# First layer norm's rstd and shift: from four GpSimd instructions to seven ScalarE instructions

## What is computed

```
h = layernorm(x) * (1 + ca) + sa
x = x + ga * mamba(h)        # in_proj, conv, silu, x_proj, softplus, selective scan, gate, out_proj
h = layernorm(x) * (1 + cb) + sb
x = x + gb * moe(h)          # one shared expert, the best of 7 routed experts
layernorm(x) = (x - mean(x)) / sqrt(var(x) + 1e-05)
```

## Time and profile before

| | |
|---|---|
| median of 3 runs | 2424.81 us (2423.86 to 2426.68) |
| profiled execution, its own time | 2425.52 us |
| span of that execution in the profile | 2423.7 us |
| PE busy | 2129.3 us, 88% |
| DVE busy | 1948.4 us, 80% |
| POOL busy | 1979.4 us, 82% |
| ACT busy | 1346.9 us, 56% |

### The profile page before, as it was taken

How to read it: one execution, slowest core, us unless ns; L and a number is a source line. 1 busy time by engine, 2 the same in 40 slices (tenths; PEclk the granted TensorE clock), 3 DMA queues, 4 the chain that set the end, 5 groups by cost and what they waited for, 6 DMA issues and landing times. The chain is left out here.

```text
span 2423.7 us, 31216 instructions
## 1 busy us (share of the span) xinstructions
PE 2129.3 (88%) x7668; PEld 1007.6 (42%) x7669; DVE 1948.4 (80%) x2114; ACT 1346.9 (56%) x2391; POOL 1979.4 (82%) x858
## 2 busy tenths in 40 slices
PE   8859898988989898989898989889875779999998
PEld 3214343443434343434343334434332456666565
DVE  4889999999999999999999999999999832222222
ACT  4657666667585767666666667675745212222221
POOL 1999999999989999999998999999899445555553
PEclk9868999899989898989899899999887889999999
DMA  6433242424242324343242424242422512222221
GB/s 175 137 101 98 78 106 65 104 74 117 77 102 72 98 74 103 83 101 103 75 111 74 108 68 117 80 103 69 98 69 53 208 42 87 86 87 85 84 85 47
DMA packets 148360, 224.35 MB, mean 93 GB/s; under 512 B 47187, under 2 KB 84577, under 8 KB 144098
## 3 DMA queue, kind: packets, MB, share of 16 engines
q1 hardware_dynamic: 134818, 182.40, 28.8%
q0 software_dynamic: 13376, 40.12, 5.5%
HBM read 99.46 MB, written 31.45 MB: 54 GB/s over the span
## 5 line engine op out<-in xcount | busy, mean ns | idle before, releaser
L1279 POOL TENSOR_TENSOR ring<-ring,reps 128x2048 f32<-128x2048 f32 x256 | 1154.7, 4530 | 42.6 <-ACT state L865 42.6
L973 DVE TENSOR_TENSOR_SCAN ring<-dA,state,ring 128x512 f32<-128x512 f32 x768 | 929.7, 1262 | 13.5 <-ACT dA L850 9.2
L850 ACT ACTIVATE dA<-d_rep,a 128x512 f32<-128x512 f32 x1024 | 690.1, 686 | 433.1 <-DVE ring L973 426.4
L1272 POOL TENSOR_TENSOR ring<-u_rep,reps 128x2048 f32<-128x2048 f32 x96 | 436.2, 4544 | 44.6 <-PE bank L590 44.5
L960 DVE TENSOR_TENSOR ring<-u_ps,reps 128x2048 f32<-128x2048 f32 x160 | 360.5, 2269 | 8.8 <-issue 4.9
L590 PE MATMUL bank<-ring,spread 128*32 128x512 f32 x2048 | 283.2, 703 | 42.4 <-POOL ring L1279 37.8
L561 PE MATMUL bank<-n,w1s 128*128 128x512 f32 x512 | 266.1, 657 | 61.1 <-DVE delta L941 38.5
L973 DVE TENSOR_TENSOR_SCAN ring<-dA,ring 128x512 f32<-128x512 f32 x256 | 293.7, 1201 | 11.5 <-ACT dA L850 10.4
L1553 DVE TENSOR_TENSOR hid<-z,sg 128x512 f32<-128x512 f32 x70 | 48.4, 692 | 295.6 <-ACT sg L1530 295.6
L1468 PE MATMUL z<-ring,hT 128*128 x560 | 262.2, 612 | 3.6 <-issue 2.1
L516 PE MATMUL bank<-xin,w_in 128*128 128x512 f32 x512 | 244.9, 619 | 8.3 <-ACT xin L701 8.3
(11 more groups left out here) (237 smaller groups left out, 2456.7 us busy)
## 6 DMA issues: line engine op xcount, KB each, us to landing
d_rep<-delta SPq DMA_DIRECT2D x1024, 64.0 KB, 2.0
reps<-bc_rows SPq DMA_DIRECT2D x128, 256.0 KB, 6.3
u_rep<-us SPq DMA_DIRECT2D x384, 64.0 KB, 2.0
xres<-in_x SPq DMA_DIRECT2D x16, 512.0 KB, 3.6
token_rows<-xpad SPq DMA_DIRECT2D x32, 256.0 KB, 2.4
token_rows<-xres SPq DMA_DIRECT2D x16, 512.0 KB, 2.9
xin<-in_x SPq DMA_DIRECT2D x15, 512.0 KB, 9.4
ring<-in_w SPq DMA_DIRECT2D x7, 1024.0 KB, 14.5
```

The source lines that it names most:

```text
L850: nc.scalar.activation(dA[:, u % ABANK, :], d_rep[:, q, :], ACT.Exp, scale=t["a"][:, u:u + 1]).then_inc(da_ready, 1)
L973: nc.vector.tensor_tensor_scan(hs[:, s % RING, g, :], dA[:, u % ABANK, :], hs[:, s % RING, g, :], state[:, u:u + 1] if m else 0.0, ALU.mul ...
L1272: nc.gpsimd.tensor_tensor(hs[:, s % RING], u_rep[:, i % UBUF, :].unsqueeze(1).to_broadcast([P, NG, T]), b_rep[:, par, :].rearrange("p (g t ...
L1279: nc.gpsimd.tensor_tensor(hs[:, s % RING, :, :], hs[:, s % RING, :, :], c_rep[:, par, :].rearrange("p (g t) -> p g t", g=NG), ALU.mult).th ...
```

## The change

`rstd` and `shift` of the first layer norm are computed by ScalarE. `rstd` becomes `exp(-0.5 * ln(var + eps))`: an Ln with eps as its bias, an Exp with scale -0.5; the mean is negated by a Copy, and `shift` is made by four Copies of one column each, since their scale is a column of `rstd`. The new piece is V, at set 11, tile 0 of `evict`; piece R leaves `gps`. In the start, `deviation(0)` stands ahead of the silu of `c`, and `deviation(1)` behind the load of the exponential table. `mhalf` gets a wider tile, whose upper half holds eps. The list `transfers` is only broken into lines differently.

```
-            11: [[], [], [], [(('B', 2), -1)]],
+            11: [[(('V', 0), 2)], [], [], [(('B', 2), -1)]],
...
-            8: [(('IN', 13), 0), (('R', 0), 2), (('G0', 0), -1)],
+            8: [(('IN', 13), 0), (('G0', 0), -1)],
...
+            def deviation(f):
+                act.wait_ge(stats_ready, f + 1)
+                if known(f) and f == 0:
+                    act.wait_ge(zeroed, 5)
+                nc.scalar.activation(rstd[:], mv[:, :, 1], ACT.Ln, bias=eps[:, 0:1]).then_inc(rstd_step, 1)
+                nc.scalar.activation(mv[:, :, 0], mv[:, :, 0], ACT.Copy, scale=-1.0).then_inc(rstd_step, 1)
+                act.wait_ge(rstd_step, 3 * f + 2)
+                nc.scalar.activation(rstd[:], rstd[:], ACT.Exp, scale=-0.5).then_inc(rstd_step, 1)
+                act.wait_ge(rstd_step, 3 * f + 3)
+                for tt in range(TT):
+                    last = nc.scalar.activation(shift[:, tt:tt + 1], mv[:, tt, 0:1], ACT.Copy, scale=rstd[:, tt:tt + 1])
+                last.then_inc(shift_ready, 1)
...
+            exp_table()
             act.wait_ge(a_loaded, 16)
             nc.scalar.activation(t["a"][:], t["a"][:], ACT.Exp).then_inc(a_exp, 1)
+            deviation(0)
             act.wait_ge(c_loaded, 16)
             nc.scalar.activation(cs, cT, ACT.Silu).then_inc(c_silu, 1)
             normalize(0)
...
                     exp_table()
+                    deviation(1)
                     act.wait_ge(selectors, 1 + NF)
...
-            def rsqrt(f):
-                hold(pool, stats_ready, f + 1, held)
-                nc.gpsimd.tensor_scalar(mv[:, :, 1], mv[:, :, 1], EPS, None, ALU.add).then_inc(rstd_step, 1)
-                nc.gpsimd.tensor_scalar(mv[:, :, 0], mv[:, :, 0], -1.0, None, ALU.mult).then_inc(rstd_step, 1)
-                hold(pool, rstd_step, 3 * f + 2, held)
-                nc.gpsimd.tensor_tensor(rstd[:], mv[:, :, 1], t["mhalf"][:, 0:TT], ALU.pow).then_inc(rstd_step, 1)
-                hold(pool, rstd_step, 3 * f + 3, held)
-                nc.gpsimd.tensor_tensor(shift[:], mv[:, :, 0], rstd[:], ALU.mult).then_inc(shift_ready, 1)
...
-            rsqrt(0)
-            rsqrt(1)
```

More of the change, by code:

```diff
@@ L118, in fused_program @@
         mv2, rstd2, shift2 = sb("mv2", [P, TT, 2]), sb("rstd2", [P, TT]), sb("shift2", [P, TT])
+        eps = t["mhalf"][:, TT:TT + 1]
         xpad, us, res = t["xpad"], sb("us", [P, 2, KI, T]), sb("res", [P, 2, KI, T])
@@ L255, in fused_program @@
             15: []}
-        transfers = [('W2', 0), ('ACC2', 0), ('U', 5), ('D', 4), ('XR', 0), ('D', 6), ('U', 7), ('D', 5), ('D', 8), ('U', 10), ('WO', 0), ('D', 7),
-                     ('U', 13), ('D', 10), ('D', 9), ('BC', 0), ('X', 0), ('D', 11), ('ROWS', 0), ('D', 12), ('D', 13), ('D', 15), ('D', 14), ('LOG', 0),
-                     ('U', 15), ('D1', 0), ('U1', 2), ('D1', 2), ('D1', 1), ('D1', 3)]
+        transfers = [('W2', 0), ('ACC2', 0), ('U', 5), ('D', 4), ('XR', 0), ('D', 6), ('U', 7), ('D', 5), ('D', 8), ('U', 10), ('WO', 0), ('D', 7), ('U', 13), ('D', 10), ('D', 9),
+                     ('BC', 0), ('X', 0), ('D', 11), ('ROWS', 0), ('D', 12), ('D', 13), ('D', 15), ('D', 14), ('LOG', 0), ('U', 15), ('D1', 0), ('U1', 2), ('D1', 2), ('D1', 1), ('D1', 3)]
         FIRST_TRANSFERS = [("D", 0), ("D", 1), ("D", 2), ("U", 2), ("D", 3)]
@@ L802, in lump @@
                     logs(f, int(kind[1]))
+                elif kind == "V":
+                    deviation(f)
                 elif kind == "N":
@@ L1303, in body @@
                         do(item, c, m)
-            nc.gpsimd.memset(t["mhalf"][:], -0.5).then_inc(zeroed, 1)
+            nc.gpsimd.memset(t["mhalf"][:, 0:TT], -0.5).then_inc(zeroed, 1)
+            nc.gpsimd.memset(eps, EPS).then_inc(zeroed, 1)
             nc.gpsimd.memset(t["ident"][:], 0.0).then_inc(zeroed, 1)
@@ L1308, in _ @@
             nc.gpsimd.memset(xpad[:, :, 0:KCONV - 1], 0.0).then_inc(zeroed, 1)
-            pool.wait_ge(zeroed, 4)
+            pool.wait_ge(zeroed, 5)
             nc.gpsimd.affine_select(out=t["ident"][:], in_=t["ident"][:], compare_op=ALU.not_equal, fill=1.0,
@@ L1580, in build @@
                 "spread": spread, "gather": spread[:, 0, :], "state": sb("state", [P, NSET * NG]), "xpad": sb("xpad", [P, KI, T + KCONV - 1]),
-                "mhalf": sb("mhalf", [P, TT]),
+                "mhalf": sb("mhalf", [P, 2 * TT]),
                 "a": sb("a", [P, NSET * NG]), "cb": sb("cb", [P, KI]),
```

2 lines of the change are left out of this document (removed).

## The result

The changed kernel is slower, as forecast: 2438.15 us (median of 5, 2436.60 to 2439.48), where the kernel before ran 2424.77 us beside it. The ratio is 1.0054, 95% interval 1.0039 to 1.0069, so +13.4 us; forecast were +17.6 (2442.4 us). The profiled execution took 2439.48 us, its span is 2437.6 us, 13.9 more than before.

The account below looks back on a forecast made before the run. VectorE was taken as the bound, hanging on ScalarE at one point of the chunk. Loop 16.5 + start 2.3 - chunk 0's 1.2 = 17.6 us, giving 2442.4 us; range 2426 to 2450, the forecast's own 2438 to 2449.2.

Parts of the forecast that it names:

- The path: Chunks 1 to 13: V delays ScalarE's table loads, set 11's save, GpSimd's weighing, TensorE's sum and VectorE's gate multiply, 1.27 us each chunk.
- ScalarE's block: Table loads and silus in chunk 7, 943.26 to 949.58: 6.3 us without any `dA`, after which VectorE, GpSimd and TensorE hang.
- GpSimd's wait: Before set 11, for the state ScalarE saves: forecast to grow from 0.64 by 2.09 and 1.27 to near 4.0 us.
- the bound from below: Loop cost with V at 1.23 us (Ln as cheap as plain, free waits): 13 x 1.12 = 14.6 us.
- ScalarE's slack: Up to tile 47's `dA`, ahead of the table loads: 0.11 us, so 1.38 of V leaves 1.27 us delay.
- The wait at tile 50: VectorE's scan waiting for `dA` after the table loads: forecast 0.57 + 1.27 - 0.78 = 1.06 us instead of 0.57.
- The waiting sum: VectorE's 1.41 us wait for TensorE's sum at 960.56 can't absorb the delay, as the sum moves by the same 1.27.
- the rival that the wait absorbs it all: VectorE's 1.41 us wait for the sum hides the 1.27; only start and chunk 0 count: 2425.9 us, chance 0.12.
- The start: Before the first scan: late silu of `c` delays TensorE's first matmuls by 3.34 and transposes by 2.3 us; 2.3 counted.
- Chunk 0: GpSimd works without a gap there, so its relief lets set 11 start earlier: 1.2 us gained, once.
- GpSimd as the bound: Rival: every chunk bound by GpSimd's work, V hidden in ScalarE's idle time, 29.3 us gained: 2397.8 us, chance 0.07.
- The dearest V: Rival: seven instructions without overlap plus two waits, 2.50 us a chunk in ScalarE's loop: 2458 us, chance 0.06.

Follow-up runs that it names:

- the load alone: Kernel before, R kept on GpSimd, plus seven idle instructions of V's kinds and waits at V's place on ScalarE: 2438.28 us, ratio 1.0055.
- the relief alone: Kernel before without R in the loop and nothing added on ScalarE; chunks 2 to 15 use chunk 1's `rstd` and `shift`: 2421.99 us, 0.9987.
- the turned entry: Kernel before with VectorE's first layer norm statistics ahead of the second sum's gate multiply at set 10, tile 1: 2423.69 us, 0.9999.
- the loop alone: Kernel before with V on ScalarE and no R on GpSimd in the chunks, start left on GpSimd: 2436.24 us, ratio 1.0048.
- the start alone: Changed kernel's start (first two layer norms on ScalarE), chunks as in the kernel before with R on GpSimd: 2426.07 us, 1.0008.
- silu first: Changed start with silu of `c` ahead of `deviation(0)`, two more table loads, chunks as in the kernel before: 2423.05 us, 0.9995.
- two kernels with V behind the block: Changed kernel with V moved to set 12, tile 3, ahead of piece N: 2440.79 us; same with the gate's exponential ahead of both: 2440.93 us.

## Why the prediction was right, and where its sizes were off

**The path was right.** VectorE hangs on ScalarE's block: the load alone gives the cost of the loop, the relief alone gave 2.0 us. As a bound for the whole chunk VectorE was said too broadly: the turned entry took 7.8 us of its waits for sums away and gained nothing, with TensorE ahead of it in set 10. The marks that the forecast set: V 1.2 to 1.9 us (1.41), waits for `dA` twice a chunk of about 0.8 and 1.1 (0.71 and 0.86), GpSimd's wait 4.0 (3.99), transposes near 14.1 (14.34), a chunk 1.3 longer (16.55 / 13 = 1.27 between the two profiles, 14.2 / 13 = 1.10 by the times of the load alone). Two of these meet by luck. GpSimd's wait was 2.88 with the relief alone, 0.15 over the 0.64 + 2.09, and the block came 1.11 late instead of 1.27; the errors cancel. And 1.27 holds chunk 1 with 1.97 us, which was 0.26 longer under the load alone and 0.17 shorter in the loop alone; between the same two scans these runs lost 14.2 and 13.7 us.

**The time lay at the edge.** 2438.15 us is the lower end of the forecast's own range (2438 to 2449.2). The load's 14.2 us even lie below what was given as the bound from below, 14.6, since that bound moved only V's price and kept the slack at 0.11.

**V itself** was taken at 1.38 and measured 1.41. The overlap of 0.09 between neighbours and the wait for an own result, 0.03, carried over. The 0.03 was called ScalarE's own, but was read from a scan on VectorE; the rows now show it on ScalarE (L771 ends at 946.03, L773 starts at 946.06). The Trainium skill's budget of about 0.3 us for an ACTIVATE with a column as bias ("ScalarE: Activation LUTs", section "Rules for kernel authors") would have made it 2.1 us, an estimate, had it been V's price. The trace has 1.41 us, as each instruction overlaps the next. The same page (section "What ACT_TABLE_LOAD costs") gives 186 ns and 93 more for a column operand. The trace agrees: the plain Copy took 193 ns, the Copies with a column 279.

**The mis-sized term is ScalarE's slack,** taken as 0.11 us. From tile 44's `dA` to the table load the stretch grew by 6.22 - 5.11 = 1.11, so of V's 1.41 some 0.30 were absorbed. The prediction said that ScalarE ran without gaps from 940.20 on. It didn't. These are its rows in the kernel before:

```profile
940.83 0.58 ACT L745 ACTIVATE xpad<-bank 128x512 f32<-128x512 f32 x1
941.37 0.69 ACT L850 ACTIVATE dA<-d_rep,a 128x512 f32<-128x512 f32 x1
942.00 0.58 ACT L745 ACTIVATE xpad<-bank 128x512 f32<-128x512 f32 x1
942.55 0.69 ACT L850 ACTIVATE dA<-d_rep,a 128x512 f32<-128x512 f32 x1
```

From an eviction to the next `dA` are 0.54 and 0.55 us (940.83 to 941.37, 942.00 to 942.55); in the changed kernel, where ScalarE is late and never waits, they are 0.48 both times (948.99 to 949.47, 950.08 to 950.56). The two `dA` had waited some 0.06 for a scan: by the step of 1.17 the scans of tiles 45 and 46 end at 941.35 and 942.52, 0.02 ahead of them. From tile 47's `dA` to the table load the stretch was 3.06 us (940.20 to 943.26) and is 2.87 (948.38 to 951.25), 0.19 shorter; with the 0.11 that makes the 0.30. The wait at tile 50 follows from this: 0.57 + 1.11 - 0.71 = 0.97 by this working, 0.86 by the row; the rest is VectorE, which was itself slightly late.

**The waiting sum gives a little, and not in every chunk.** It was said that its 1.41 us can absorb nothing. The sum did start as late as forecast: from the scan of tile 50 to 963.15 are 4.86 us, as before (4.85). VectorE's wait for it was 1.18 instead of 1.41 in chunk 7 because TensorE then took 5.08 us for it instead of 5.34. With that, chunk 7 is longer by 0.92 us and not by 1.11. Other chunks differ more. In chunk 6 the waits for `dA` grow from 0.6 to 1.6 us and those for sums from 1.2 to 2.3: the chunk is 2.26 longer. In chunk 8 the former grow from 0.9 to 1.8, but the latter fall from 2.7 to 0.9, and 0.7 for `u_ps` is new: it is 0.17 longer. The loop alone and the load alone show the same in these chunks (2.21 and 2.18, 0.14 and 0.15), so this is no scatter. The rival that the wait absorbs it all (2425.9 us) is refuted for the whole, but in chunk 8 it is nearly right. What makes one chunk absorb and another not is open.

**The start** was forecast at 2.3. The first scan came 3.0 later in this pair of profiles and 1.4 with the start alone, and by the times the start alone costs 2.0: the size was right as far as can be told. That TensorE's first matmuls waited for the silu of `c` is shown by silu first, where the order is turned and the loss is gone.

**Chunk 0** was forecast at -1.2 for the relief. The relief alone measured -2.0; in its profile chunk 0 is 2.25 us shorter. Between the two profiles before and after chunk 0 is 4.8 us shorter. The relief is not all of that: with R kept and only the load added, chunk 0 was 2.8 us shorter too (first scan 0.63 later, next chunk 2.13 earlier), with the start alone 1.1, and with both load and relief only 2.3. These don't add up, and why chunk 0 shortens under a load alone is open.

**The sum.** By the times: load 14.2 (forecast 16.5), relief -2.0 (-1.2), start 2.0 (2.3), together 14.2, against 17.6 forecast and 13.4 measured for the whole. The term that was mis-sized is the load's: 1.27 a chunk forecast and 1.10 measured, 13 x 0.17 = 2.2. In chunk 7 the slack explains it (1.11). Over all chunks it is less neat: in the profile of the load alone, chunks 1 to 3 are 0.7 us longer each and chunks 4 to 13 1.22 each, between 0.15 and 2.18.

**The rivals.** GpSimd as the bound is refuted by the relief alone (2421.99, not near 2397.8). The dearest V is refuted by its length, 1.41 instead of 2.50.

## What to carry to other kernels

An engine that is a third idle can still be full where it matters. Ask of a moved instruction not which engine has time, but which idle stretch of that engine it would stand in, and who waits for what is queued behind it, on every engine and down to a reciprocal of 0.18 us: with the start untouched, the same move cost 12.2 us in one place and 3.0 in another.

When work is taken from an engine, look at its waits first. GpSimd was 94% busy and stood still three times a chunk for another engine; from chunk 4 on, all that it was spared it waited.

To size a cost, halve the change: load without relief, relief without load. Each of the two is read against the kernel before, and each has its own interval, here 2 to 3 us to either side; if their sum meets the whole more closely, that is luck.

## What the runs showed that was not expected

TensorE's granted clock moves with the waits, and the sums move with it. The same 32 matmuls of a sum, in the kernel before and then in the changed one (columns as in the answer to the earlier trace rows; the granted clock is the third from the end):

```profile
154.97:161.31 6.34, 6.34 (x33) 1.65 (x34) 2.48 (x3) 2.08 (x3) 6.34 (x2) 0.57 0.01 3
640.89:644.53 3.64, 3.64 (x33) 1.04 (x33) 3.64 (x3) 1.94 (x4) 3.64 (x2) 1.00 0.54 164
955.15:960.49 5.34, 5.34 (x33) 1.36 (x34) 4.00 (x4) 3.56 (x10) 5.34 (x2) 0.68 0.00 0
```

```profile
154.67:159.52 4.85, 4.85 (x33) 1.26 (x34) 3.71 (x4) 2.70 (x5) 4.85 (x2) 0.74 0.02 3
963.15:968.23 5.08, 5.08 (x33) 1.22 (x34) 3.98 (x4) 3.55 (x10) 5.08 (x2) 0.71 0.00 0
```

A sum takes 3.64 us where the granted clock stays at the upper level, 2.4 GHz, and 6.34 in the slowest of these rows, where it spends most of the stretch at the lower one, 1.2 GHz. The sum at 640.89 follows matmuls without a gap; the others stand behind a wait of TensorE (1.84 us ahead of the one at 154.97, 0.62 ahead of the one at 154.67). Ahead of the one at 955.15, TensorE had waited 2.85, 0.41 and 0.82 us within 10 us, and the granted clock was already 0.55 from 948.60 to 952.00. The length of the last wait doesn't order them, though. In chunk 0, two sums went from 5.80 and 6.34 to 5.00 and 4.85, but the first one went from 5.34 behind a wait of 4.49 us to 6.49 behind one of 3.65. The three together are 1.1 us shorter; that this is part of the 4.8 us by which the chunk became shorter is not shown.

Over chunks 1 to 14 it goes the other way: the granted clock is 0.90 instead of 0.92, and TensorE needs 30.8 us more for the same matmuls. Is this the cause of the loss? The runs speak against it as the main one. The two kernels with V behind the block and the changed start have a mean clock of 0.912 over their whole execution and lose 16.7 and 16.6 us, the changed kernel has 0.906 and loses 13.4 (0.917 before). How much of the 13.4 us the slower matmuls add in single chunks, the runs don't separate. A single chunk of a single profile doesn't tell what a change of 1 us is worth: here the same delay made one chunk 0.17 us longer and another 2.26.
